# The second convolution's first gathers issued before the last two node tiles' rows are stored, with the head, the seam and the selection rounds reordered

## The chip, the cores and the metric

The kernel runs on one core of a Trainium2 chip. The metric is the device time of one execution in microseconds. The kernel before took 2100.82 us (median of 3 runs, 2099.37 to 2104.38).

## What is computed

A graph network and a feed-forward layer over 6250 nodes of width 256, with 100,000 weighted edges whose destinations are sorted, all in float32. Cut to what matters:

```python
def gcn(x, W, b): return segment_sum(w[:, None] * (x @ W)[src], dst) + b
f1 = layernorm(x)
h  = gcn(f1, W1, b1)                                  # first convolution
z  = leaky(concat([h, f1[root]]))
z  = leaky(gcn(z, W2, b2))                            # second convolution
x  = x + leaky(concat([z, h[root]]) @ Wl + bl)
y  = layernorm(x)
weights = y @ wr + br
sel = top_k(weights, 3125)[:3124]                     # routed nodes
out = x + y; out[sel] += weights[sel] * (gelu(y[sel] @ w1 + b1) @ w2 + b2)
```

## The kernel before

**Tiles and windows.** The nodes lie in 49 windows of 128 (`NW`), the edges in 784 tiles of 128 (`NT`, the last two unused). Four tiles are a group (`TG`), four groups an iteration of 16 tiles (`RING`), and there are 49 iterations (`NIT`) in each of the two convolutions. Both run from the last edges to the first, so from the highest nodes down. For each tile GpSimd gathers the source rows (128 rows of 1 KB) with one indirect DMA (L360) into `ring`, which holds 8 groups. VectorE builds a selection matrix `S` (L1012: destination in the window equals column, times edge weight). TensorE multiplies `S` by the gathered rows and sums a group's four tiles in PSUM (`sums`, L613, `edge_group`), and VectorE adds the sum to the window's slot in `acc` (`add_last`, L1020). Where a group's edges reach into a lower window, an extra sum with `S_more` follows. A float32 product shows as two MATMUL records in the trace.

**Order within a convolution.** POOL may write group g of the ring when `group_used` has reached g - 6 (L355). VectorE raises it once in each group, behind the add of the sum before. `edge_round` is VectorE's part of one iteration, with the selects made two groups ahead; `rounds` on each engine is the loop. The first `first` iterations (here one) are edges alone, then each iteration carries the steps of one finished window, one between each two groups. In the first convolution these are: stage the sums (L433), turn them (L679), multiply by W1 (L703, `ps_h`), bias (L459), leaky (`z_step0`), multiply by W2 (L694, `ps_o`), copy to `rows` (L449) and store to `conv_rows` in HBM (L452), which the second convolution gathers from. In the second they are the same turn, Wl, the residual and layernorm (`x1_step`, `norm_rows`), the router's weight and the FFN's up (L737) and down (L726) products.

**Head.** GpSimd gathers the first 8 groups from the raw `x`; their row statistics are taken (`row_stats`, L952) and the rows scaled in the ring: the first batch (14 tiles) by POOL (L349), the second (16 tiles) by ACT (L414). Meanwhile x is loaded in six chunks (`XCH`), normalised by ACT (L403) and POOL (L345), and stored as `normed_rows` (L286), from which all later gathers of the first convolution read. SyncE then reads the root's row (L293), loads x again (L296, L298) and the late weights Wl, fw1 and fw2 (L304). `fw1s` and `fw2s` (`staged_a`, `staged_b`) are scratch for edges and statistics before. `first_root_row` computes the root's share of the second convolution, between the first iteration and the others.

**Seam.** After the first convolution's last iteration (window 1's and window 0's steps are left, `rounds(..., NW)` and `second_layer(NW)` on TensorE) POOL waits until all rows are stored: `t2_stored` counts 16 at the start and 16 for each store, and L335 wants 16 * (NW + 2). TensorE computes the root terms (L602, L718), VectorE `rootrow` (L1156, L1158).

**Tail.** When the last windows are done, the 3124 largest weights are found by a search in 8 rounds (`ROUNDS`): VectorE counts (L1245, L1246), TensorE adds the counts over partitions (L869). Behind each count TensorE runs pieces of the remaining FFN (`last_ffn`, 26 pieces): two before round 0, one behind rounds 0 and 1, two behind each other, the rest at the end. Then VectorE adds the routed FFN result to the output, from the highest windows down (L1280), and SyncE stores it in 9 chunks (L308); the chunk of windows 2 to 4 waits for the last piece.

## Time and profile before

| | |
|---|---|
| median of 3 runs | 2100.82 us (2099.37 to 2104.38) |
| profiled execution | 2107.75 us, span 2106.0 us |
| TensorE matmul / weight load | busy 1686.5 us (80%) / 1351.4 us (64%) |
| VectorE / ACT | busy 1136.2 us (54%) / 373.3 us (18%) |
| GpSimd (POOL) | busy 1514.8 us (72%) |
| bytes moved | 242 MB, mean 115 GB/s |

```profile
## 2 busy tenths in 40 slices
PE   1588876777767776766689999999998989898886
DVE  8666454444434333333266666665665656555556
POOL 7677777777777777777477777777777777777730
PEclk9999898898988888788699999999999999999998
```

Each digit is the busy share of a slice of 52.7 us in tenths. PE is TensorE, DVE VectorE, ACT ScalarE, PEclk the clock that TensorE was granted. POOL shows 7 nearly everywhere, because its issue between two gathers isn't counted as busy. The seam is the 4 in the middle of POOL's line, the tail the 3 and 0 at its end.

### The profile page before, as it was taken

The page shows a single profiled execution, that of the slowest core. Times are in us where ns is not written, and L with a number is a line of the kernel's source. Part 1 is how long each engine was busy: PE and PEld are TensorE (multiplying, and loading weights), DVE is VectorE, ACT ScalarE, POOL GpSimd, SP SyncE. Part 2 cuts the span into 40 slices and gives each one's busy share as a digit, 9 for nine tenths or more (in the row PEclk, how much of TensorE's full clock was granted, in tenths as well). Part 3 has the DMA queues.
Part 4 walks back from the last instruction along what each step waited for, and adds up shares of the span by engine and source line. Part 5 has one row for each costly group of instructions (what it writes and reads, how often), then busy time and mean ns, then how long its engine had stood idle before and what let it go on. Part 6 is the DMA issues. An engine that isn't in the chain of part 4 may idle for free.

```text
span 2106.0 us, 39360 instructions
## 1 busy us (share of the span) xinstructions
PE 1686.5 (80%) x7147; PEld 1351.4 (64%) x7148; DVE 1136.2 (54%) x4017; ACT 373.3 (18%) x921; POOL 1514.8 (72%) x1609
## 2 busy tenths in 40 slices
PE   1588876777767776766689999999998989898886
PEld 0466655655545555554468888877887777677665
DVE  8666454444434333333266666665665656555556
ACT  6211000001000000000012222222222222222221
POOL 7677777777777777777477777777777777777730
PEclk9999898898988888788699999999999999999998
DMA  8933333333333333333233333333333333333313
GB/s 270 316 112 110 112 110 111 110 110 111 109 112 112 110 112 109 112 112 110 78 105 105 103 105 105 104 103 104 103 105 104 104 105 104 104 104 104 104 57 122
DMA packets 113372, 242.23 MB, mean 115 GB/s; under 512 B 29013, under 2 KB 62740, under 8 KB 113338
## 3 DMA queue, kind: packets, MB, share of 16 engines
q0 software_dynamic: 75200, 205.10, 33.9%
q1 hardware_dynamic: 28444, 29.03, 4.3%
q10 hardware_dynamic: 9694, 7.77, 1.2%
q14 instruction: 27, 0.22, 0.0%
q8 instruction: 7, 0.11, 0.0%
HBM read 222.42 MB, written 19.38 MB: 115 GB/s over the span
## 4 chain that ended last, share of the span: by engine, by line
POOL 44%; PE 25%; issue 18%; DVE 7%; DMA 3%; DVEq 2%; ACT 0%; ACTq 0%; POOLq 0%
POOL ring L360 44%; PE ps_agg L613 15%; PE ps_up L737 3%; PE ps_dn L726 3%; DMA ring<-normed_rows,idx 2%; DMA ring<-conv_rows,idx 1%; DVE S L1012 1%; PE ps_o L694 1%; DVE xs L1280 1%; DVE fw2s L934 1%; DVE acc L1020 1%; PE ps_dn L724 1%; PE ps_o L691 1%; PE ps_o L772 1%; DVE fw2s L952 0%
## 5 line engine op out<-in xcount | busy, mean ns | idle before, releaser
L613 PE MATMUL ps_agg<-ring,S 128*128 x3136 | 863.5, 424 | 363.7 <-DVE S L1012 136.0
L613 PEld LDWEIGHTS ps_agg<-ring,S 128*128 128x128 f32 x3136 | 639.3, 210 | 526.7 <-issue 433.7
L360 POOL DMA_INDIRECT ring<-conv_rows,idx x782 | 747.6, 956 | 256.7 <-issue 232.8
L360 POOL DMA_INDIRECT ring<-normed_rows,idx x752 | 718.0, 955 | 239.6 <-issue 221.0
L1020 DVE TENSOR_TENSOR acc<-acc,ps_agg x490 | 206.4, 421 | 621.5 <-PE ps_agg L613 571.5
L1012 DVE TENSOR_SCALAR S<-iota,dstc,wc 128x128 f32<-128x128 int16 x1584 | 448.7, 363 | 157.3 <-issue 125.8
L613 PE MATMUL ps_agg<-ring,S_more 128*128 x768 | 197.6, 403 | 20.1 <-DVE S_more L1012 13.8
L726 PE MATMUL ps_dn<-fw2s,hT 128*128 128x256 f32 x848 | 209.1, 401 | 0.0
L613 PEld LDWEIGHTS ps_agg<-ring,S_more 128*128 128x128 f32 x768 | 153.4, 204 | 58.7 <-issue 35.5
L726 PEld LDWEIGHTS ps_dn<-fw2s,hT 128*128 128x128 f32 x848 | 163.5, 199 | 40.3 <-issue 18.9
L737 PE MATMUL ps_up<-xnT,fw1s 128*128 128x256 f32 x800 | 183.1, 382 | 1.5 <-ACT hT L471 1.5
L737 PEld LDWEIGHTS ps_up<-xnT,fw1s 128*128 128x128 f32 x800 | 148.1, 190 | 19.7 <-ACT hT L471 1.6
L433 ACT ACTIVATE stage<-acc 128x256 f32 x98 | 40.8, 416 | 426.7 <-DVEq L1046 414.8
L1012 DVE TENSOR_SCALAR S_more<-iota,dmore,wc 128x128 f32<-128x128 int16 x384 | 109.7, 363 | 8.6
L471 ACT ACTIVATE hT<-ps_up,fb1c 128x256 f32<-128x256 f32 (+1 forms) x212 | 82.2, 474 | 67.1 <-PE ps_up L737 67.1
L443 ACT ACTIVATE xnT<-ps_t 128x256 f32<-128x256 f32 x49 | 18.8, 384 | 414.1 <-PE ps_t L679 414.1
L1002 DVE SCALAR_TENSOR_TENSOR zT<-yT 128x256 f32<-128x256 f32 x99 | 42.1, 425 | 39.3 <-DVE acc L1020 31.7
L694 PE MATMUL ps_o<-W2s,zT 128*128 128x256 f32 x200 | 61.2, 432 | 0.3 <-DVE zT L1002 0.3
L459 ACT ACTIVATE yT<-ps_h,b1c 128x128 f32<-128x128 f32 x98 | 30.7, 364 | 155.4 <-PE ps_h L703 153.2
L478 ACT ACTIVATE acc<-ps_dn 128x256 f32 (+1 forms) x53 | 20.4, 384 | 200.2 <-PE ps_dn L726 200.2
L703 PEld LDWEIGHTS ps_h<-xnT,W1s 128*128 128x128 f32 x392 | 53.3, 197 | 3.1
L703 PE MATMUL ps_h<-xnT,W1s 128*128 128x128 f32 x392 | 53.0, 279 | 0.0
(211 smaller groups left out, 1028.3 us busy)
## 6 DMA issues: line engine op xcount, KB each, us to landing
ring<-conv_rows,idx POOLq DMA_INDIRECT x782
ring<-normed_rows,idx POOLq DMA_INDIRECT x752
conv_rows<-rows ACTq DMA_DIRECT2D x50, 128.0 KB
xs<-in_x SPq DMA_DIRECT2D x4, 1280.0 KB, 18.2
normed_rows<-xs SPq DMA_DIRECT2D x3, 1280.0 KB, 6.9
xs<-in_x SPq DMA_DIRECT2D x4, 896.0 KB, 15.7
out_rows<-xs SPq DMA_DIRECT2D x3, 1024.0 KB
xs<-in_x SPq DMA_DIRECT2D x2, 1152.0 KB
```

The source lines that it names most:

```text
L360: pool.indirect_dma_start(out=ring[:, slot * TG + t, :], out_offset=None, in_=rows_of, in_offset=bass.IndirectOffsetOnAxis(ap=idx[:, tile: ...
L433: nc.scalar.activation(stage[:, :], flat(acc[:, ds(slot, 1), :]), ACT.Copy).then_inc(staged[l], 1)
L459: last = nc.scalar.activation(yT[:, k, :], ps_h[:, k * P:(k + 1) * P], ACT.Identity, bias=b1c[:, k:k + 1])
L471: last = nc.scalar.activation(hT[:, b * HB + c, 0:tokens], ps_up[:, c, 0:tokens], ACT.Gelu_apprx_tanh, bias=fb1c[:, b * HB + c:b * HB + c ...
L613: last = nc.tensor.matmul(to, select[:, t, :], moving, start=(t == 0), stop=(t == TG - 1))
L694: last = nc.tensor.matmul(ps_o[:, 0:D], zT[:, k, :], W2s[:, k, :], start=False, stop=(k == KC - 1))
L703: last = nc.tensor.matmul(ps_h[:, c * P:(c + 1) * P], W1s[:, k, c * P:(c + 1) * P], aggT[:, k, :], start=(k == 0), stop=(k == KC - 1))
L726: last = nc.tensor.matmul(ps_dn[:, 0:D], hT[:, c, window * P:(window + 1) * P], fw2s[:, c, :], start=False, stop=(c == HC - 1))
L737: last = nc.tensor.matmul(ps_up[:, c, 0:tokens], fw1s[:, k, (b * HB + c) * P:(b * HB + c + 1) * P], of[:, k, :], start=(k == 0), stop=(k = ...
L1002: return V.scalar_tensor_tensor(to, of, SLOPE, of, ALU.mult, ALU.max)
L1012: last = V.tensor_scalar(to[:, t, :], iota[:, 0:P], at, wc[:, ds(column, 1)], ALU.is_equal, ALU.mult)
L1020: V.tensor_tensor(to, to, flat(ps_agg[:, ds((i + 1) & 1, 1), 0:D]), op=ALU.add).then_inc(acc_step[l], 1)
```

## The change

- **Gathers of the second convolution.** Its ring starts in the half that the first convolution's last iteration doesn't use. The first 14 gathers (`FIRST_TILES`) read through `idx_far`, in which each source below 256 (`NEAR`, windows 0 and 1) is replaced by a zero row, and wait only for the stores down to window 2. Rows of windows 0 and 1 in `conv_rows` are zeroed at the start by three stores from ACT. From group 4 on POOL waits for all stores.
- **Adding the missing rows.** The sources of these edges are loaded to all partitions (`near_src`, 868 KB, on SyncE in the place of the late weights). VectorE makes two one-hot masks of 128 x 1792 in `first_root_row`, one for window 0 and one for window 1. In the seam TensorE multiplies them by the rows of the two windows (28 products), and VectorE adds the results to the 14 ring tiles (`patched`). The first group of the second convolution waits for that. `fw1s` and `fw2s` hold the masks, so they load after the last patch, and TensorE waits for them after the first iteration (`late_weights_in`); Wl loads early.
- **Seam order.** The loops of the first convolution end one window sooner; window 1's product with W2 comes before window 0's turn, and window 0's product goes to `ps_dn` and from there to `row_of_0`. The selects for the second convolution's first two groups come before the patch adds.
- **Head order.** x is loaded and stored in nine chunks instead of six. VectorE makes the first selects before the second batch's row statistics; half of these come before the first iteration, half after it with their factors. The first batch's scaling is shared by POOL (parts 0 and 2) and ACT (parts 1 and 3), with a semaphore for each.
- **Selection.** One FFN piece behind every count instead of one or two.

The diff, cut to its core:

```diff
+        near_src = hT[:, :, :].rearrange("p c n -> p (c n)")[:, 0:FIRST_SPAN]
+        row_of_0 = hT[:, HC - 1, :]
+        near_hot = [staged_a[:, 0:FIRST_SPAN], staged_b[:, 0:FIRST_SPAN]]
...
-        XCH = [(39, NW), (29, 39), (19, 29), (14, 19), (7, 14), (0, 7)]
+        XCH = [(39, NW), (29, 39), (24, 29), (19, 24), (14, 19), (10, 14), (7, 10), (3, 7), (0, 3)]
-        BY_POOL = range(4, len(XCH))
-        STORES = [0, 1, 4, 2, 3, 5]
+        BY_POOL = range(5, len(XCH))
+        STORES = [0, 1, 2, 5, 3, 6, 4, 7, 8]
...
# SyncE
-            for to, of in big_loads[2:]:
+            sp.wait_ge(spread_done, 1)
+            sp.dma_start(near_src[:, 0:E - FIRST_EDGE].bitcast(i32), src[FIRST_EDGE:E].rearrange("(o n) -> o n", o=1).to_broadcast([P, E - FIRST_EDGE])).then_inc(near_loaded, 16)
+            sp.dma_start(*big_loads[2]).then_inc(last_layer_loaded, 16)
+            for done in patched:
+                sp.wait_ge(done, 1)
+            for to, of in big_loads[3:]:
                 sp.dma_start(to, of).then_inc(late_weights, 16)
...
# GpSimd
                 if l == 1:
-                    pool.wait_ge(t2_stored, 16 * (NW + 2))
+                    pool.wait_ge(far_ready, 1)
+                    pool.wait_ge(zero_stored, 16 * 3)
+                    pool.wait_ge(t2_stored, 16 * NW)
...
-                    slot = g % SLOTS
+                    slot = (g + l * QG) % SLOTS
+                    early = l == 1 and it == 0
+                    if early:
+                        pool.wait_ge(group_used[0], NG - SLOTS + q + 2)
+                    if l == 1 and g == QG:
+                        pool.wait_ge(t2_stored, 16 * (NW + 2))
...
# ACT
+            rounds((stage_step0, turned_step0, rows_step0, y_step0), NW - 1)
+            rows_step0(NW - 1)
+            stage_step0(NW - 1)
+            turned_step0(NW - 1)
+            y_step0(NW - 1)
+            act.wait_ge(o_done[0], NW + 2)
+            act.wait_ge(near_ready, 1)
+            nc.scalar.activation(row_of_0, ps_dn[:, 0:D], ACT.Copy).then_inc(o_kept[0], 1)
+            act.wait_ge(o_kept[0], NW + 2)
+            act.dma_start(t2_dram[0:P, :], row_of_0).then_inc(t2_stored, 16)
...
# TensorE
+            pe.wait_ge(near_ready, 1)
+            for q in range(QG):
+                if q >= 2:
+                    pe.wait_ge(patched[q - 2], 1)
+                for t in range(q * TG, min(q * TG + TG, FIRST_TILES)):
+                    bank, half = patch_banks[q & 1][t % TG // 2], t % 2
+                    edges = slice(t * P, (t + 1) * P)
+                    nc.tensor.matmul(bank[:, half * D:(half + 1) * D], near_hot[1][:, edges], rows[:, :], start=True, stop=False)
+                    last = nc.tensor.matmul(bank[:, half * D:(half + 1) * D], near_hot[0][:, edges], row_of_0, start=False, stop=True)
+                    if half:
+                        last.then_inc(patch_done, 1)
...
-                for _ in range(1 if r < 2 else 2):
-                    next(pieces, None)
+                next(pieces)
...
# VectorE
+                if l == 0:
+                    first_selects(0)
+                    for q in range(2):
+                        row_sums(1, q)
                 dve.sem_inc(acc_step[l], 1)
...
+                if l == 0:
+                    with dve.Fori(0, 1) as it:
+                        edge_round(l, it, None)
+                    row_factors(1, [row_sums(1, q) for q in range(2, QG)][-1])
+                    with dve.If(1 < d):
+                        with dve.Fori(1, d) as it:
+                            edge_round(l, it, None)
...
# in first_root_row
+                dve.wait_ge(near_loaded, 16)
...
+                dve.wait_ge(raw_second, 2)
+                for hot, of in zip(near_hot, (lane_at, lane_next)):
+                    last = V.tensor_scalar(hot, near_src.bitcast(i32), zeros[:, 0:1], of, ALU.max, ALU.is_equal)
+                last.then_inc(near_ready, 1)
...
+            first_selects(1)
+            for q in range(QG):
+                tiles = range(q * TG, min(q * TG + TG, FIRST_TILES))
+                dve.wait_ge(landed[1][q], 16 + NIT // 2 * LAND + 16 * len(tiles))
+                for b in range(len(tiles) // 2):
+                    dve.wait_ge(patch_done, 2 * q + b + 1)
+                    held = flat(ring[:, RING + tiles[2 * b]:RING + tiles[2 * b] + 2, :])
+                    last = V.tensor_tensor(held, held, patch_banks[q & 1][b], op=ALU.add)
+                last.then_inc(patched[q], 1)
```

## Rows read from the trace of the kernel before

**Rows 1.** The page: busy time, the chain that ended last, the costliest groups.

```profile
PE 1686.5 (80%) x7147; PEld 1351.4 (64%) x7148; DVE 1136.2 (54%) x4017; ACT 373.3 (18%) x921; POOL 1514.8 (72%) x1609
...
POOL 44%; PE 25%; issue 18%; DVE 7%; DMA 3%; DVEq 2%; ACT 0%; ACTq 0%; POOLq 0%
...
L360 POOL DMA_INDIRECT ring<-conv_rows,idx x782 | 747.6, 956 | 256.7 <-issue 232.8
```

**Rows 2.** Timeline of the head: start us, us, engine, line, operation, operands, count, [idle before].

```profile
57.88 5.32 DVE L952 BATCH_NORM_STATS2 fw2s<-ring 128x6 f32<-128x256 f32 x16
...
67.91 7.97 ACT L414 ACTIVATE ring<-ring,fw2s 128x256 f32<-128x256 f32 x16 [14.35 <-DVEq L958]
69.51 3.17 DVE L1012 TENSOR_SCALAR S<-iota,dstc,wc 128x128 f32<-128x128 int16 x12 [1.69 <-issue]
71.23 6.76 PE L613 MATMUL ps_agg<-ring,S 128*128 x16 [54.05 <-DVE S L1012]
...
75.36 0.42 DVE L1020 TENSOR_TENSOR acc<-acc,ps_agg  x1 [0.92 <-PE ps_agg L613]
...
76.20 0.99 POOL L360 DMA_INDIRECT ring<-normed_rows,idx  x1 [10.73 <-DVEq L1042]
...
78.24 3.09 SPq L298 DMA_DIRECT2D xs<-in_x  x2
...
82.96 0.42 DVE L1020 TENSOR_TENSOR acc<-acc,ps_agg  x1 [0.27 <-issue]
...
85.34 0.41 DVE L1123 COPY rootrow<-ps_dn 1x256 f32<-1x256 f32 x1 [1.21 <-PE ps_dn L602]
...
87.17 0.42 DVE L1020 TENSOR_TENSOR acc<-acc,ps_agg  x1 [0.39 <-issue]
...
91.41 0.95 POOL L360 DMA_INDIRECT ring<-normed_rows,idx  x1 [0.30 <-issue]
```

**Rows 3.** Two source lines: duration ns min/median/max, first and last start us, shapes.

```profile
L916 DVE TENSOR_SCALAR fw1s<-fw1s x1: 693/693/693, 6.0 to 6.0; 98x1024 f32<-98x1024 int32 x1
...
L972 DVE TENSOR_SCALAR hT<-ident,gcol x4: 254/310/477, 14.6 to 15.2; 98x98 f32<-98x98 f32 x4
```

**Rows 4.** Stretches of the head: us, busy by engine, granted clock, DMA share, GB/s.

```profile
96.00:99.00 3.00, 3.00 (x15) 2.26 (x14) 1.83 (x6) 0.77 (x2) 2.09 (x4) 1.00 1.08 356
99.00:102.00 3.00, 3.00 (x19) 2.77 (x18) 1.71 (x6) 0.63 (x2) 2.39 (x3) 1.00 0.62 190
```

**Rows 5.** Timeline of the seam, columns as in rows 2.

```profile
1039.78 0.36 ACTq L452 DMA_DIRECT2D conv_rows<-rows  x1
...
1041.78 0.94 POOL L360 DMA_INDIRECT ring<-conv_rows,idx  x1 [18.69 <-DMA conv_rows<-rows]
...
1049.10 3.78 PE L613 MATMUL ps_agg<-ring,S 128*128 x8 [6.26 <-DMA ring<-conv_rows,idx]
...
1057.39 1.89 PE L613 MATMUL ps_agg<-ring,S_more 128*128 x8
```

**Rows 6.** Stretches of seam and second convolution: PE, PEld, DVE, ACT, POOL, clock, DMA.

```profile
1027.00:1030.00 3.00, 1.70 (x4) 0.79 (x3) 0.42 (x1) 0.23 (x1) 0.00 (x0) 0.50 0.00 0
...
1057.00:1060.00 3.00, 2.28 (x11) 1.67 (x9) 1.74 (x6) 0.00 (x0) 2.39 (x3) 0.99 0.37 98
...
1100.00:1200.00 100.00, 97.36 (x459) 82.63 (x459) 67.53 (x249) 24.92 (x63) 75.92 (x80) 1.00 0.36 104
```

**Rows 7.** Timeline: the add that frees group 24's ring slot, and group 24's gather.

```profile
1138.49 0.42 DVE L1020 TENSOR_TENSOR acc<-acc,ps_agg  x1 [0.28 <-issue]
...
1159.99 0.95 POOL L360 DMA_INDIRECT ring<-conv_rows,idx  x1 [0.30 <-issue]
```

**Rows 8.** Timeline of the tail: a count of round 1, second up, last down.

```profile
2053.79 0.61 PE L869 MATMUL ps_o<-ring,ones 105*128 105x15 f32 x2 [0.44 <-DVE ring L1246]
...
2070.43 3.72 PE L737 MATMUL ps_up<-xnT,fw1s 128*128 128x256 f32 x16 [1.53 <-ACT hT L471]
...
2081.73 19.48 DVE L1280 SCALAR_TENSOR_TENSOR xs<-acc,ring,xs 128x256 f32<-128x256 f32 x49
```

More of the change, by code:

```diff
@@ L347, in _ @@
                         pool.wait_ge(raw_stats, 1)
-                        for t in RAW_TILES[0]:
-                            last = nc.gpsimd.tensor_scalar(ring[:, t, :], ring[:, t, :], raw_rstd[:, t:t + 1], raw_nmr[:, t:t + 1], ALU.mult, ALU.add)
-                            if t % TG == TG - 1 or t == RAW_TILES[0][-1]:
-                                last.then_inc(raw_first, 1)
+                        for part in range(0, QG, 2):
+                            for t in RAW_TILES[0][part * TG:(part + 1) * TG]:
+                                last = nc.gpsimd.tensor_scalar(ring[:, t, :], ring[:, t, :], raw_rstd[:, t:t + 1], raw_nmr[:, t:t + 1], ALU.mult, ALU.add)
+                            last.then_inc(raw_first[part], 1)
                         for stored in f_stored:
@@ L411, in _, with scale_rows @@
             normalise_rows(1)
+            def scale_rows(tiles):
+                for t in tiles:
+                    last = nc.scalar.activation(ring[:, t, :], ring[:, t, :], ACT.Identity, scale=raw_rstd[:, t:t + 1], bias=raw_nmr[:, t:t + 1])
+                return last
+            act.wait_ge(raw_stats, 1)
+            for part in range(1, QG, 2):
+                scale_rows(RAW_TILES[0][part * TG:(part + 1) * TG]).then_inc(raw_first[part], 1)
             act.wait_ge(raw_stats, 2)
-            for t in RAW_TILES[1]:
-                last = nc.scalar.activation(ring[:, t, :], ring[:, t, :], ACT.Identity, scale=raw_rstd[:, t:t + 1], bias=raw_nmr[:, t:t + 1])
+            last = scale_rows(RAW_TILES[1])
             last.then_inc(raw_second, 1)
@@ L708, in _ @@
                 pe.sem_inc(s, 1)
-            rounds(0, (no_step, turn_step0, h_step0, no_step), NW, first_root_term)
-            second_layer(NW)
-            pe.wait_ge(late_weights, 16 * (N_WEIGHTS - 2))
+            rounds(0, (no_step, turn_step0, h_step0, no_step), NW - 1, first_root_term)
+            second_layer(NW - 1)
+            turn_sums(0, NW - 1)
+            h_step0(NW - 1)
+            nc.tensor.matmul(ps_dn[:, 0:D], ones[0:1, :], rootrow[0:1, :], start=True, stop=False)
+            pe.wait_ge(z_ready[0], NW + 1)
+            for k in range(KC):
+                last = nc.tensor.matmul(ps_dn[:, 0:D], zT[:, k, :], W2s[:, k, :], start=False, stop=(k == KC - 1))
+            last.then_inc(o_done[0], 1)
+            pe.wait_ge(o_kept[0], NW + 2)
+            pe.wait_ge(near_ready, 1)
[9 more added lines that the diff above has]
+                        last.then_inc(patch_done, 1)
+            pe.wait_ge(last_layer_loaded, 16)
             pe.wait_ge(root_taken, 2)
@@ L997, in _ @@
             node_stats(1)
-            row_stats(0)
-            row_stats(1)
+            row_factors(0, [row_sums(0, q) for q in range(QG)][-1])
             def leaky(to, of):
@@ L1116, in _ @@
             dve.wait_ge(edges_kept, 3)
+            lane_at, group_at, lane_in, lane_next = (lane[:, i:i + 1] for i in range(4))
             def first_root_row():
```

98 lines of the change are left out of this document (64 added, 34 removed).

## Prediction

> **What bounds the kernel now.** I read the page first. GpSimd (POOL) is 72% busy, nearly all of it in L360: 1564 indirect gathers, one for each tile of 128 edges in each convolution. One is busy for 0.956 us, the next starts 1.26 us after it. TensorE has more busy time, but in the chain of work that ended last POOL holds 44% and TensorE 25% [rows 1]. The timeline of POOL then shows two long gaps: 10.73 us in the head, for a used ring group, and 18.69 us in the seam between the convolutions, for the store of the last conv2 row [rows 2, 5]. Between them it never stops. So the time is: head until the first gather from the normed rows (76.20), 752 gathers, seam, 782 gathers, and a tail of some 79 us. An edit is worth what it moves of POOL's next gather, or takes from head, seam or tail. One thing has to be watched: in 1100 to 1200 TensorE is busy for 97.4 of 100 us [rows 6], so work pushed onto it in the seam can come back as a full ring.
>
> **Part 1, the head.** Removed: the first sums' wait for the statistics of the second raw batch. Added: these statistics and factors between first and second iteration, ACT's scaling behind them, and the mask work in first_root_row. I follow VectorE, which all wait for. The first batch's factors end at 57.9. Before, the selects (69.51) came 1.6 to 1.7 after the second factors (67.9, when ACT starts), so they start at 59.6 now. Eight at 3.17/12 take 2.1 (61.7), eight row statistics at 5.32/16 take 2.7 (64.4), and only then acc_step lets TensorE start. Before, its first group started at 71.23 and the add that waited for it at 75.36, 4.1 later; now that add is at 68.5 and done at 68.9 (before 75.8). POOL follows 0.4 behind: 69.3 instead of 76.20, 6.9 us earlier [rows 2]. The rows are stored by then: SyncE reads one of them at 65.2, and the finer chunks start storing sooner. POOL's six fewer scalings save nothing more, its wait is for the used group.
> That lead doesn't last. Groups 8 to 10 need used-counts of the first iteration, but group 11 needs VectorE's first add of the second. POOL reaches group 11 at 69.3 + 12 x 1.26 = 84.4. VectorE ends the first iteration at 68.9 + (83.4 - 75.8) = 76.5. Then come some 0.6 of loop end, 8 statistics (2.7) and the factors (4.7, from 63.2 to 67.9): 84.5. ACT scales 16 tiles in 7.97 [rows 2]: 92.5. first_root_row now waits for that, because its second mask overwrites the scratch of these factors. Queued behind the wait are, on VectorE, the masks and all selects and adds of the second iteration, and behind these TensorE and group 11. The small operations for indices and lanes fit before 92.5.
> The two masks are tensor_scalars of 128 x 1792 with per-partition scalars. The nearest rows: 1024 columns of int32 with constants took 0.693, 98 float columns with such a scalar 0.254 at best [rows 3]; the selects, 128 columns from int16, follow at 0.264 each [rows 2]. The first two fit about two columns a cycle of 0.96 GHz behind a fixed part, the select fits one. Bounds are 1.0 and 2.0 us for a mask; I take 1.05, since the masks read int32 and write float as L916 does. VectorE goes on at 94.6. From the end of first_root_row (85.75) to the end of the next add (87.59) it was 1.84: 96.4, POOL at 96.8. Group 11 started at 91.41 before [rows 2]. **The head costs 5.4 us**: 12.4 of new waiting against 6.9 gained. Range +4.5 to +11.
> On the masks the Trainium skill, "VectorE: DVE Perf Modes" (section on the perf-mode tier table), says that a float32 tensor_scalar with source and result in SBUF runs at twice the base rate. L972 and L916 agree with it, the int16 selects don't get it. By the selects' rate the sum would be 1.9 us longer.
> The masks also wait for a broadcast load of 868 KB, queued on SyncE behind the second load of x (6.4 MB, issued by 81.3 [rows 2]). Before, three weight loads (2.6 MB) stood there, and they were in at about 99, when the traffic fell from 356 to 190 GB/s [rows 4]. At some 250 GB/s beside the gathers they need 10 us of that, so x is in at some 88 and the broadcast at 91. It hides behind ACT's scaling with 1.5 us of cover; beyond that it costs one for one.
>
> **Part 2, the seam.** The first 14 gathers of conv 2 no longer wait for the last two windows, only for 48 stores, the last issued at 1021.6. A store took 2.0 us from issue (1039.78) to POOL's restart (1041.78) [rows 5]: they start at 1023.6 and end at 1023.6 + 14 x 1.26 = 1041.2. Rows of the last two windows read a zero row instead, at the same cost per gather. From group 4 on POOL waits for all stores. That end is reordered: the product of window 1 (some 3.3 with its ones row, at the low clock) now stands before the turn of window 0, and ACT copies and stores it before it stages window 0. Staging moves 3 us, but window 0's h waited behind that product before, so h moves only 0.8: row 0 is stored at 1040.6 and seen by POOL at 1042.6. The fifteenth gather was at 1041.78 + 17.6 = 1059.4: lead 16.8.
> TensorE has 28 one-hot products to add, from 1040.6. A product is two MATMULs of 256 columns. Eight took 3.78 at 1049 and 1.89 at 1057 [rows 5], so 0.95 or 0.5 a product. The granted clock was 0.50 from 1027 and had risen in 1057 to 1060 [rows 6]. I take 5 us at the lower level (5.3 products) and 22.7 x 0.5 = 11.4: end at 1057.0. Bounds: 14 us (all fast) and 26.6 us (all slow). VectorE's seven adds of 512 columns (0.42 for 256, so some 0.7) run beside it, the last ends 0.8 behind. The Trainium skill, "TensorE: Matmul & The Clock Gate" (Part 1), calls the throttled clock the default, which activity releases; the rows of 1049 and 1057 agree. Without that release the sum is 10 us longer.
> Then the root terms, 3.0 us (before 3.9 at half clock): 1060.0. Four selects and the empty add 1.5, four selects and the next add 1.8: 1063.3. POOL's group 8, which by itself would come at 1042.6 + 20.2 = 1062.8, starts at 1063.7; before, at 1041.78 + 30 x 1.26 = 1079.6. **The seam gives 16.0 us.**
> What is late next? fw1s and fw2s now load after the last patch (1057.8), 2.1 MB beside the gathers: at 356 - 110 = 246 GB/s [rows 4] 8.6 us and 2 of latency, 1068.4; at most 16 us (81.5 to 99 before, with 2.6 MB and a backlog), 1074. TensorE needs them after its first iteration, 5 groups from 1060.3 in some 11.5 us: 1071.8. Hidden by 3.4 us. Then the ring: least slack was at group 24, which started at 1159.99 while the add that frees it ended at 1138.91: 21.1 us [rows 7]. POOL's lead uses 16.0, TensorE's later second iteration up to 4: 20.0. It holds, by one microsecond.
>
> **Part 3, the tail.** One piece of the last FFN behind every count instead of two in rounds 2 to 7. A round with one piece takes 2.94, so the rounds, which ended at 2077.0, end some 3 us sooner; but the pieces of up (L737: 3.72 for two at full clock [rows 8]) now stand in rounds 6 and 7 and hold back the next count by some 1.4. The final adds start near 2080 instead of 2081.73. Sixteen pieces are left instead of ten: from the second up to the end it was 22.8 us (2070.43 to 2093.26), less 1.3 for counts between: 2078.6 to 2100.1. The last 5 windows' adds wait for that and end at 2102.5 instead of 2101.2, but their store is short, while before the span ended 4.8 us behind the last add, for the queue of stores. **I cost the tail at 0**, from -2.6 (clock up throughout) to +2.5 (down through the rounds).
>
> **The sum.** +5.4 - 16.0 + 0 = -10.6. The profiled execution took 2107.75 (span 2106.0 and 1.75 around it), 6.9 more than the median of the runs, 2100.82. So the span should be 2095, the profiled execution 2097, and the median 2100.8 - 10.6 = 2090.2, which I round to 2091.
>
> **The rivals.** First, **the broadcast load is late** and not ACT: it stands behind 6.4 MB, and the gathers start 6.9 us earlier beside it; against it, 1.5 us of cover. It can reach 99: 2090.5 + 6.5 = 2097.
> Second, **slower: the products don't pass**. If TensorE stays at the lower clock and the hand-over of PSUM banks with VectorE makes a product 1.2 us instead of 0.95, 28 take 33.6, end at 1074, and group 8 comes at 1080.5, later than before; the ring's 21.1 us are then used up by TensorE's delay. That is 2100.8 + 5.4 + 0.9 + 1 = 2108. The seam's gain is zero from products that end at 1073. For it: the clock was low for 30 us before 1057 though TensorE worked; against it: it rose once the work closed up.
> Third, **the head is free**: if VectorE's block ended before 84.4, POOL would keep its 6.9: 2100.8 - 6.9 - 16.0 = 2078. That needs 12 us of error in one chain.
> Fourth, **it doesn't do what it says**: POOL isn't released before the last stores. Then only the head's cost is left, 2106. Little in its waits speaks for it.
> Fifth, **the tail's upper end**, 2093.5.
>
> **Chances.** Forecast 0.52 (own range 2085 to 2096), late load 0.14, products 0.12, free head 0.07, no release 0.07, tail 0.08. A measurement here tells about 0.3% (6.3 us) from no change, so faster is under 2094.5, slower over 2107.1. Faster: 0.47 + 0.02 + 0.07 + 0.06 = 0.62. Slower: 0.09 and 0.04 for two of the losses together, 0.13. Same: the rest, 0.25. The range from 2083 to 2106 leaves out the free head and the products.
>
> **What would show it.** Head: first gather from normed rows near 69, then one POOL wait of about 12 us ending near 97, with ACT's 16 scalings just before the two masks; if the masks follow a DMA, the first rival holds, and without a second wait the third. Seam: 14 gathers from 1029, a gap of under 2 us before the fifteenth and of about 1 us before group 8, and 56 MATMULs into ps_up, ps_h and ps_o in 16 to 17 us; if POOL waits for used groups again within 200 us, the 1 us of slack was gone. Tail: counts 2.9 us apart, the last adds waiting for ps_dn. The whole is wrong if gathers start more than 1.26 us apart.

## The result and the profile after

The changed kernel takes **2096.39 us** (median of 10 runs, 2092.58 to 2102.34); the kernel before, beside it, 2100.48 (10 runs, 2098.72 to 2104.38). The ratio is 0.9981, with a 95% interval of 0.9973 to 0.9989: 4.1 us faster, where I had forecast 9.8. The time lies in the range, the sign is right, the size is not: less than half of it came.

The profiled execution took 2095.7 us (span 2094.0). Its page, against [rows 1]:

```profile
PE 1689.6 (81%) x7203; PEld 1359.1 (65%) x7204; DVE 1141.9 (55%) x4030; ACT 375.5 (18%) x927; POOL 1509.1 (72%) x1603
...
POOL 42%; PE 29%; issue 18%; DVE 4%; DMA 4%; DVEq 2%; SPq 1%; ACT 0%; ACTq 0%; POOLq 0%
...
L385 POOL DMA_INDIRECT ring<-conv_rows,idx x768 | 734.6, 957 | 241.7 <-issue 225.4
```

A gather costs what it did, and POOL still leads the chain. TensorE's share of it rose from 25 to 29%, the first sign that POOL waits for it somewhere. The head, against [rows 2] (columns as there):

```profile
68.26 0.98 POOL L385 DMA_INDIRECT ring<-normed_rows,idx  x1 [6.82 <-DVEq L1119]
...
80.63 0.36 SPq L316 DMA_DIRECT2D hT<-in_src  x1
...
83.59 7.96 ACT L444 ACTIVATE ring<-ring,fw2s 128x256 f32<-128x256 f32 x16 [23.47 <-DVEq L1031]
...
90.19 0.15 DVE L1219 CAST lane<-search 128x1 f32<-128x1 int32 x1 [2.85 <-issue]
...
92.30 1.21 DVE L1227 TENSOR_SCALAR fw1s<-hT,vrow,lane 128x1792 f32<-128x1792 int32 x1 [1.77 <-DMA hT<-in_src]
93.43 1.21 DVE L1227 TENSOR_SCALAR fw2s<-hT,vrow,lane 128x1792 f32<-128x1792 int32 x1
94.55 1.11 DVE L1084 TENSOR_SCALAR S<-iota,dstc,wc 128x128 f32<-128x128 int16 x4
95.58 0.41 DVE L1092 TENSOR_TENSOR acc<-acc,ps_agg  x1
...
94.52 0.94 POOL L385 DMA_INDIRECT ring<-normed_rows,idx  x1 [10.62 <-DVEq L1119]
```

The first gather from the normed rows comes 7.9 us earlier, and the eleventh group 3.1 later (94.52 against 91.41). The masks wait for the broadcast load, not for ACT, which is done at 91.55. And POOL starts before the add at 95.58: its release (DVEq) comes from VectorE's queue, ahead of the engine. The seam, against [rows 5]:

```profile
1023.77 0.94 POOL L385 DMA_INDIRECT ring<-conv_rows,idx_far  x1 [0.30 <-issue]
...
1051.56 0.59 PE L777 MATMUL ps_h<-hT,fw1s 128*128 128x256 f32 x2
...
1053.68 0.69 PE L785 MATMUL ps_dn<-rootrow,ones 1*128 1x256 f32 x2 [0.57 <-DVE rootrow L1272]
1057.86 5.79 PE L658 MATMUL ps_agg<-ring,S 128*128 x16 [3.48 <-DVE acc L1092]
...
1062.30 0.95 POOL L385 DMA_INDIRECT ring<-conv_rows,idx  x1 [1.27 <-DVEq L1119]
```

The gap of 18.69 us is gone, and group 8 comes at 1062.30 instead of 1079.70. Then, against [rows 7], where no wait stood:

```profile
1080.26 3.78 PE L658 MATMUL ps_agg<-ring,S_more 128*128 x8 [3.75 <-DVE S_more L1084]
...
1085.75 5.51 PE L793 MATMUL ps_dn<-fw2s,hT 128*128 128x256 f32 x16
...
1094.02 0.94 POOL L385 DMA_INDIRECT ring<-conv_rows,idx  x1 [1.80 <-DVEq L1119]
1111.48 0.94 POOL L385 DMA_INDIRECT ring<-conv_rows,idx  x1 [1.63 <-DVEq L1119]
1132.51 0.94 POOL L385 DMA_INDIRECT ring<-conv_rows,idx  x1 [1.18 <-DVEq L1119]
1149.54 0.42 DVE L1092 TENSOR_TENSOR acc<-acc,ps_agg  x1 [0.28 <-issue]
1149.85 0.95 POOL L385 DMA_INDIRECT ring<-conv_rows,idx  x1 [2.57 <-DVEq L1119]
```

POOL waits for used groups: 7.0 us in five waits between 1090 and 1150, of which four stand here (each number in brackets holds the usual 0.30 of issue). The DVE line is the add that frees group 24's slot, and the gather below it is group 24's. In the tail the counts are 2.94 us apart, and the span ends 77.6 us behind the last gather instead of 79.5.

### The profile page after: what moved, and what is told of

It reads as the page before. It is cut to its first block, busy times and chain, and to the rows that moved or that the text cites. A ratio compares the mean times of both kernels' runs of the same rounds, so it can differ in the third digit from the quotient of the medians.

```text
span 2094.0 us, 39574 instructions
## 1 busy us (share of the span) xinstructions
PE 1689.6 (81%) x7203; PEld 1359.1 (65%) x7204; DVE 1141.9 (55%) x4030; ACT 375.5 (18%) x927; POOL 1509.1 (72%) x1603
## 4 chain that ended last, share of the span: by engine, by line
POOL 42%; PE 29%; issue 18%; DVE 4%; DMA 4%; DVEq 2%; SPq 1%; ACT 0%; ACTq 0%; POOLq 0%
POOL ring L385 41%; PE ps_agg L658 16%; PE ps_dn L793 4%; PE ps_up L804 4%; DMA ring<-normed_rows,idx 2%; DVE S L1084 1%; DMA ring<-conv_rows,idx 1%; PE ps_o L743 1%; PE ps_dn L791 1%; SPq L312 1%; PE ps_o L839 1%; DVE acc L1092 1%; DMA hT<-in_src 1%; PE ps_o L740 1%; DVEq L1092 0%
## 5 line engine op out<-in xcount | busy, mean ns | idle before, releaser
L658 PE MATMUL ps_agg<-ring,S 128*128 x3136 | 852.7, 421 | 333.9 <-DVE S L1084 87.7
L385 POOL DMA_INDIRECT ring<-conv_rows,idx x768 | 734.6, 957 | 241.7 <-issue 225.4
L470 ACT ACTIVATE stage<-acc 128x256 f32 (+1 forms) x98 | 40.8, 416 | 410.1 <-DVEq L1123 403.6
L1074 DVE SCALAR_TENSOR_TENSOR zT<-yT 128x256 f32<-128x256 f32 x99 | 42.1, 425 | 40.5 <-DVE acc L1092 31.0
L743 PE MATMUL ps_o<-W2s,zT 128*128 128x256 f32 x196 | 57.3, 416 | 0.0
## 6 DMA issues: line engine op xcount, KB each, us to landing
xs<-in_x SPq DMA_DIRECT2D x6, 640.0 KB, 15.6
```

The source lines that it names most:

```text
L385: pool.indirect_dma_start(out=ring[:, slot * TG + t, :], out_offset=None, in_=rows_of, in_offset=bass.IndirectOffsetOnAxis(ap=at, axis=0)) ...
L470: nc.scalar.activation(stage[:, :], flat(acc[:, ds(slot, 1), :]), ACT.Copy).then_inc(staged[l], 1)
L658: last = nc.tensor.matmul(to, select[:, t, :], moving, start=(t == 0), stop=(t == TG - 1))
L743: last = nc.tensor.matmul(ps_o[:, 0:D], zT[:, k, :], W2s[:, k, :], start=False, stop=(k == KC - 1))
L1074: return V.scalar_tensor_tensor(to, of, SLOPE, of, ALU.mult, ALU.max)
```

## The experiments

For the study I cut every profiled execution at POOL's gathers: head up to group 11; the 740 gathers from there to the last of the first convolution; seam from that gather to group 8 of the second; from there to the last gather; tail. The waits are those for used groups between group 8 and 1160 us. (after_again, masks_at_seam and half_products have one more, of 1.3 us, between 1232 and 1239.) All in us, from starts in POOL's timeline:

| kernel | group 11 | 740 gathers | seam | to last gather | waits | tail | span |
|---|---|---|---|---|---|---|---|
| before | 91.4 | 930.7 | 57.6 | 946.8 | 0 | 79.5 | 2106.0 |
| after | 94.5 | 928.0 | 39.8 | 954.0 | 7.0 | 77.6 | 2094.0 |
| before_again | 90.9 | 929.6 | 57.3 | 945.8 | 0 | 82.7 | 2106.4 |
| after_again | 95.9 | 929.0 | 40.6 | 956.5 | 8.8 | 77.4 | 2099.5 |
| before_light | 90.9 | 929.6 | 54.6 | 945.8 | 0 | 79.5 | 2100.5 |
| before_light_2 | 90.9 | 929.3 | 54.8 | 945.2 | 0 | 78.9 | 2099.1 |
| after_light | 94.9 | 929.6 | 39.7 | 953.9 | 7.0 | 77.6 | 2095.6 |
| half_products | 97.3 | 930.8 | 41.7 | 949.3 | 0 | 78.4 | 2097.4 |
| seam_alone | 96.0 | 930.7 | 40.7 | 947.9 | 0 | 77.4 | 2092.8 |
| root_early | 95.5 | 929.4 | 40.6 | 948.8 | 2.1 | 77.6 | 2091.9 |
| filler | 95.0 | 929.9 | 41.5 | 949.0 | 2.8 | 78.5 | 2094.1 |
| root_filler | 95.7 | 930.6 | 41.5 | 947.7 | 1.1 | 77.4 | 2092.9 |
| masks_root | 94.5 | 930.1 | 41.9 | 948.4 | 2.9 | 78.7 | 2093.6 |
| masks_at_seam | 95.8 | 930.4 | 42.1 | 957.5 | 8.0 | 82.8 | 2108.5 |
| tail_alone | 90.9 | 930.5 | 54.8 | 946.0 | 0 | 80.8 | 2103.0 |
| old_head | 91.1 | 932.5 | 41.0 | 950.8 | 2.3 | 80.2 | 2095.5 |
| old_head_best | 91.2 | 933.1 | 42.1 | 949.7 | 0 | 78.4 | 2094.6 |
| one_loop | 88.2 | 930.5 | 41.9 | 947.9 | 0.7 | 77.0 | 2085.4 |

A row shows one execution, and some stand off their kernel's median: masks_at_seam's is 7.4 us over it, old_head's 4.2, old_head_best's 7.9, and seam_alone's 5.2 under. The study's runs were taken in four sessions on three chips, each time beside the kernel before (medians 2100.62 to 2101.38); every ratio is to the kernel before of the same session, and across sessions the ratios compare better than the medians.

**Controls.** The first kernels that I made assert the bounds of the table values that TensorE and VectorE load. before_again and after_again show what that alone costs:

```diff
-v = within(pe.value_load(wtab[...]), (NW + 1) << CBITS)
+v = pe.value_load(wtab[...], min_val=0, max_val=(NW + 1) << CBITS)
```

> The kernel before, with the bounds of the table values that TensorE and VectorE load asserted (two short register instructions beside each of the 392 loads), as in all kernels of this study. Neither engine sets POOL's pace in the middle, so it should stand within 3 us of the kernel before, 2098 to 2104 us. The question is the profiled execution: the one of before took 2107.75 us against a median of 2100.8. If that was one slow execution, this profile is near 2100 us and its gathers of the first convolution run at 1.255 us from start to start instead of 1.259; if profiling itself costs 7 us, it is near 2107 again, and the 12 us between the two profiled executions are what the change brings.

> The changed kernel with the same assertions. If the change is worth the 4 us of the medians, it stands 3 to 5 us under before_again, ratio 0.998, with POOL's waits for used groups between 1090 and 1150 us again at 7 us in sum. If it is worth the 12 us that the profiled executions show, the ratio is 0.994.

before_again took 2104.4 us, ratio to before 1.0011 (1.0002 to 1.0020); after_again 2103.73, 1.0006 (0.9995 to 1.0018). By the medians the assertions cost the changed kernel 7 us and before 3 to 4; by the ratios 5 and 2. With them the change is worth 0.7 us, where 3 to 5 was expected. Of the 5.5 us between the spans of after_again and after, 1.4 stand in the head and 2.5 behind group 8. So I went on with a lighter guard, in all kernels below but half_products and masks_at_seam:

```diff
+v = within(pe.snap(pe.value_load(wtab[...]) & 0xFFFF), (NW + 1) << CBITS)
```

> The changed kernel with a lighter form of the same guard: the loaded table value is masked to 16 bits, one register instruction instead of two beside each load. The assertions of after_again cost 7 us against the changed kernel itself (2103.7 against 2096.4); the gap of VectorE ahead of its root step in the head grew from 0.7 to 6.6 us, and the waits for used groups in the second convolution from 7 to 10 us. With half the added instructions I expect half of that, 2099 to 2101 us. If it is the length of the code near the head's branches that matters and not the number of register instructions, it can come anywhere between 2096 and 2104.

> The kernel before with the light guard (one masking instruction beside each load of a table value), the partner of after_light. I expect it within 1.5 us of the kernel before itself, 2099.5 to 2102.5. Second question: both profiled executions of the kernel before so far took 7 and 4 us more than its median. If that is chance (the gathers' pace between 1.2558 and 1.2595 us, the tail between 77.4 and 82.8), this one may land anywhere in 2098 to 2106; if the profile always catches it slow, it is again 4 to 7 us over its median.

> The kernel before_light once more, for its profile. Its seam came in two lengths: 18.4 us of gap in before and before_again, with TensorE's clock at 0.50 from 1026 to 1045, and 15.3 and 15.6 in before_light and tail_alone, with the clock at 0.75 to 1.00 there. If it is chance, either may come; if the guard's form sets it, the gap is 15.3 again. The median should be 2101 to 2103.

before_light: 2102.14 us, 1.0001 (0.9991 to 1.0010), and again 2101.93, 1.0009; after_light: 2097.72, 0.9986 (0.9977 to 0.9995), less than the 2099 to 2101 expected. The pair stands 4.4 us apart by the medians and 3.2 by the ratios, against 4.1 for before and after, and is the fair one to cut up. It also shows that the seam of the kernel before has two lengths. POOL's restart in before_light, and two stretches 1025 to 1040 (us, busy by engine, granted clock, DMA), of before_light and then of before:

```profile
1037.07 0.94 POOL L360 DMA_INDIRECT ring<-conv_rows,idx  x1 [15.60 <-DMA conv_rows<-rows]
```

```profile
1025.00:1040.00 15.00, 9.13 (x34) 5.64 (x32) 5.09 (x18) 2.22 (x7) 2.32 (x3) 0.86 0.08 26
```

```profile
1025.00:1040.00 15.00, 12.54 (x32) 7.79 (x33) 1.64 (x5) 2.19 (x6) 0.00 (x0) 0.54 0.03 9
```

With TensorE's clock at 0.86 on the mean the gap is 15.6 us, at 0.54 it is 18.7. before and before_again had the long seam (18.7 both), before_light twice and tail_alone the short one (15.6, 15.8 and 15.9, clock 0.86, 0.84 and 0.77). The execution on which I based the forecast was one of the long ones.

**What fills the ring.** In half_products the 14 tiles get one product each, in root_early the root step moves ahead, in filler TensorE is kept busy:

```diff
-matmul(bank[...], near_hot[1][:, edges], rows[:, :], start=True, stop=False)
-last = matmul(bank[...], near_hot[0][:, edges], row_of_0, start=False, stop=True)
+last = matmul(bank[...], near_hot[0][:, edges], row_of_0, start=True, stop=True)
```

> The changed kernel with one product for each of the 14 first tiles instead of two: the rows of window 1 are left out of them, so the result lacks their part; the gathers, the waits and all the rest stay. Theory: the 7 us that POOL waits for used groups in the second convolution come from VectorE's first adds there, 8.8 us later than before (1062.4 against 1053.6), because they stand behind the products. Fourteen products less are 6 to 7 us of TensorE (28 took 14 us), so the adds come 6 us sooner, POOL's waits shrink from 7 to 1 or 2 us, and the whole is 5 to 6 us shorter than after_again. Rival: the later rounds of the second convolution, each with a piece of the last layers, are what uses up the ring, whenever they start; then the waits stay at 5 to 7 us and the time within 2 us of after_again.

half_products took 2098.20 us, 0.9980 (0.9971 to 0.9990): 5.5 under after_again, and the waits of 8.8 us before 1160 are gone. TensorE's work ahead of the first adds fills the ring, but this run doesn't show how much of it. Counted from POOL's group 8, VectorE's ninth add (the empty one counted) ends after 18.2 us instead of 23.2, which is the products. The tenth ends 6.0 us behind the ninth instead of 9.1, and there the clock differed too: 0.83 in 1080 to 1090, in after_again 0.73, and 0.76 in the ten us after.

```diff
 pe.wait_ge(o_kept[0], NW + 2)
+pe.wait_ge(root_taken, 2); root_term(Wls)
 ...  # products of group 0
+pe.wait_ge(rootrow_ready, 2)
+matmul(ps_dn[:, 0:D], ones[0:1, :], rootrow[0:1, :]).then_inc(root_done, 1)
 ...  # products of groups 1 to 3
```

> As after_light, but the root terms of the second convolution stand ahead of the products on TensorE, and the two copies of their row on VectorE ahead of the first two groups of patch adds, instead of behind them all. In the changed kernel 6.1 us lie between the last product (1051.8) and the first matmul of the second convolution (1057.9). Theory: half_products took the products' 7 us off and POOL's waits for used groups fell from about 10 to 2.6 us, so what counts is when VectorE's first adds come; the root step's chain of five handovers is 3 to 4 us of that, and taken out it gives 3 to 4 us of the waits back: ratio to before 0.0015 to 0.002 lower than after_light's. Rival: TensorE only gets idle later, in the second iteration, or the patch adds of group 0 wait for the root row and hold back the banks; then under 1 us.

root_early took 2094.76 us, 0.9974 (0.9963 to 0.9985), 3.0 under after_light and 0.0012 in the ratio, where 0.0015 to 0.002 was expected. Its last product, its first sums, and the one long wait that POOL has left:

```profile
1055.56 0.59 PE L780 MATMUL ps_h<-hT,fw1s 128*128 128x256 f32 x2
1056.91 1.99 PE L658 MATMUL ps_agg<-ring,S 128*128 x8 [0.76 <-DVEq L1154]
```

```profile
1148.34 0.94 POOL L385 DMA_INDIRECT ring<-conv_rows,idx  x1 [2.36 <-DVEq L1120]
```

The chain of 6 us between products and sums is down to 1. Here too the clock takes a part: counted from group 8 the ninth add ends after 20.7 us instead of 23.1 in after_light, and the tenth 5.9 us behind it instead of 8.6, with the clock at 0.83 in 1080 to 1090 instead of 0.55.

```diff
+def keep_clock():
+    with pe.If(s < 1):
+        for _ in range(7):
+            nc.tensor.matmul(ps_o[:, 0:D], ident[:, :], zeros[:, :], start=True, stop=True)
```

> after_light with seven dummy products of 256 columns (3.0 us at the full clock, into a bank that nobody reads then) on TensorE, once, in the second group of the first round with a last-layer step, where TensorE idled for 3.75 to 3.96 us from 1076.5 on and the granted clock then stood at 0.50 to 0.55 for some 10 us. Theory: that fall of the clock is 4 to 5 us of VectorE's delay (eighth to tenth add 9.2 us apart in the changed kernel, 4.1 in seam_alone, whose clock stayed at 1.00 and whose POOL never waited). With TensorE kept busy the clock stays up, POOL's waits for used groups between 1080 and 1160 fall from 7.0 to 3 us or less, and the whole is 3 to 4 us shorter than after_light. Rival: the clock falls for another reason, or the dummy products push back the group behind them by as much; then the waits stay at 6 to 8 us.

filler took 2095.11 us, 0.9967 (0.9955 to 0.9979), 2.6 under after_light. The dummy products and the step behind them, then the stretch 1080 to 1090 of filler and of the changed kernel:

```profile
1080.82 3.19 PE L692 MATMUL ps_o<-vrow,ident 128*128 128x256 f32 x14
...
1087.85 3.72 PE L800 MATMUL ps_dn<-fw2s,hT 128*128 128x256 f32 x16
```

```profile
1080.00:1090.00 10.00, 9.04 (x43) 7.45 (x42) 7.33 (x31) 1.09 (x3) 7.56 (x9) 1.00 0.36 102
```

```profile
1080.00:1090.00 10.00, 9.74 (x25) 7.60 (x26) 5.30 (x23) 1.09 (x2) 7.59 (x8) 0.53 0.37 107
```

At a clock of 1.00 the 16 matmuls take 3.72 us instead of 5.51. The ninth add comes as late as in after_light (23.0 and 23.1 us behind group 8), the tenth 4.6 us behind it instead of 8.6, and the waits fall from 7.0 to 2.8: the clock's fall behind the idle stretch had cost 4.0 us. The median fell by 2.6 where 3 to 4 was expected. seam_alone, below, shows such an execution without dummy products.

> root_early and filler together. root_early left 2.1 us of POOL's waits for used groups, with its clock at 0.83 in 1080 to 1090. If the waits have the two causes named, root step and clock, they are gone here altogether, and the time is 1 to 2 us under root_early's and 6 to 8 under before: ratio 0.9965 to 0.997. If it isn't under root_early, something else than TensorE's lateness holds POOL.

root_filler took 2093.67 us, 0.9961 (0.9947 to 0.9974), 1.1 us of waits left. Both causes together are nearly all of them. Against filler, with the clock at 1.00 in 1080 to 1090 in both, the ninth add comes 1.7 us sooner behind group 8 (21.3 against 23.0) and the waits are 1.7 us less: so much the root step brings, with the clock of its own idle stretch in it (0.83 in 1055 to 1075 in filler, 0.91 in root_filler). Without the two causes the kernel stands 8 us under before, near the 9.8 forecast.

**The head.** seam_alone puts back the old order of chunks, statistics and scaling:

> The changed kernel with the order of the head undone: six chunks of x as before, both batches of statistics and factors ahead of the first selects, POOL scaling all of the first batch. The masks stay in the head, and the seam and the selection are those of the change. Theory: the first normed gather goes back from 68 to 76 us, but the lead was lost again by the eleventh group anyway (94.5 against 91.4), which now waits for the broadcast load and the masks alone: group 11 between 93 and 95, and the whole within 2 us of after_light. Rival: the load isn't late without the early gathers beside it, group 11 comes at 91.5 to 92.5, and the whole is 2 to 4 us shorter than after_light, so that the reordered head is what takes a part of the gain.

Its first mask, its group 11 and its stretch from 1080 to 1090 (timelines and windows, columns as above):

```profile
93.83 1.21 DVE L1215 TENSOR_SCALAR fw1s<-hT,vrow,lane 128x1792 f32<-128x1792 int32 x1 [7.60 <-DMA hT<-in_src]
```

```profile
96.05 0.94 POOL L385 DMA_INDIRECT ring<-normed_rows,idx  x1 [5.47 <-DVEq L1117]
```

```profile
1080.00:1090.00 10.00, 6.83 (x32) 5.86 (x33) 7.56 (x32) 1.19 (x3) 7.65 (x8) 1.00 0.39 107
```

It took 2099.73 us, 0.9995 (0.9985 to 1.0004), 2.0 over after_light, at the edge of what was expected; the two intervals overlap. So with the masks in the head, the new order of the head gains 2 us at most. The load was later than expected (93.8), VectorE stood 7.6 us at it, and group 11 came at 96.0 instead of 93 to 95. By chance its profile shows TensorE's clock up in 1080 to 1090 and no waits for used groups; it was the fastest of its 11 runs, the median is 5 us above.

masks_at_seam moves the masks with their waits to the end of the first convolution:

```diff
 rounds(0, (z_step0, no_step, zero_step0, no_step), NW - 1, ..., first_root_row)
+dve.wait_ge(near_loaded, 16)
+...
+for hot, of in zip(near_hot, (lane_at, lane_next)):
+    last = V.tensor_scalar(hot, near_src.bitcast(i32), zeros[:, 0:1], of, ALU.max, ALU.is_equal)
```

> The changed kernel with the two masks, and the waits for the broadcast load and for the scaled raw rows, taken out of the head and put on VectorE ahead of the last turn of the first convolution, where it has idle time. Theory: POOL's second wait in the head (10.6 us, until 94.5) hangs on ACT's scaling, the masks and the selects behind them in one chain. Without the masks (2.4 us, with their gap 3) and with the first iteration's end no longer behind the load (0.7 us), group 11 starts 3 to 4 us sooner, near 91, and the whole is 3 to 4 us shorter than after_again, since the ring's stalls in the second convolution start from the seam and move along. Rival: the scaling by ACT alone sets it, since TensorE waits for it anyway; then group 11 moves by the masks' 2.4 us at most, and if the masks at the seam delay the last store, half of that is lost again.

A miss: 2102.88 us, 1.0006 (0.9995 to 1.0017), 0.9 under after_again. Group 11 in masks_at_seam, then in after_again:

```profile
95.76 0.95 POOL L385 DMA_INDIRECT ring<-normed_rows,idx  x1 [12.28 <-DVEq L1119]
```

```profile
95.95 0.95 POOL L385 DMA_INDIRECT ring<-normed_rows,idx  x1 [12.59 <-DVEq L1119]
```

Two masks less, 2.4 us of VectorE, moved POOL by 0.2. In both kernels the small operations ahead were done at 93.1 to 93.2; from there VectorE's queue took 2.6 to 2.8 us to reach the report of the used group, with masks or without. What counted was when the small operations came, and those stood behind a gap: 6.6 us of VectorE ahead of the root step. (In the changed kernel itself that gap is 0.7, another of 2.85 stands behind the root step, and the load came last, at 92.3.)

> root_early with the masks at the end of the first convolution, as in masks_at_seam. There group 11 of the head came at 95.8 against 95.9 with the masks in the head: the 2.4 us of masks cost 0.2, because VectorE's queue, which reports the used groups, needs 2.5 us for the instructions behind them in any case. In this lighter form VectorE may reach the masks earlier than the broadcast load, as in the changed kernel (waits 1.8 us for it, until 92.3): then the head gains 1 to 2 us over root_early. Rival: the gap of VectorE without a cause in the profile (2.9 and 6.6 us so far) takes it, and nothing is gained.

masks_root took 2096.48 us, 0.9979 (0.9969 to 0.9989), no better than root_early, the gap still there:

```profile
88.90 0.16 DVE L1075 SCALAR_TENSOR_TENSOR root_in<-rootcol 128x2 f32<-128x2 f32 x1 [6.50 <-issue]
```

one_loop is masks_root with filler and without code that these edges never run:

```diff
 row_factors(1, [row_sums(1, q) for q in range(2, QG)][-1])
-with dve.If(1 < d):
-    with dve.Fori(1, d) as it:
-        edge_round(l, it, None)
```

> masks_root with filler, and without the second copy of VectorE's loop over the rounds without steps (its range is empty for these edges, so nothing that runs is left out, only the code that is jumped over). In after_light, root_early, masks_root and root_filler VectorE stands still for 6.5 us between the factors' last step (82.4 to 83.2) and the root step (89 to 89.7), and the profile names no cause. Theory: that is the fetch of its instructions behind the jump, while 6.4 MB of x are loading; without the copy the gap is under 1.5 us, the root step comes at 83 to 84, and group 11 of the head at 88 to 90. TensorE's second iteration still waits for ACT's scaling (91.4), so group 12 is what counts: 95 to 96 instead of 100, and the whole 3 to 5 us under masks_root. Rival: VectorE waits for something else there (the root column's load); then the gap stays at 6 us and nothing is gained.

Its root step, and POOL's waits in the head:

```profile
82.60 0.16 DVE L1082 SCALAR_TENSOR_TENSOR root_in<-rootcol 128x2 f32<-128x2 f32 x1 [0.15 <-DVE fw2s L1003]
```

```profile
88.20 0.94 POOL L385 DMA_INDIRECT ring<-normed_rows,idx  x1 [4.84 <-DVEq L1127]
95.36 0.94 POOL L385 DMA_INDIRECT ring<-normed_rows,idx  x1 [2.35 <-DVEq L1127]
100.76 0.94 POOL L385 DMA_INDIRECT ring<-normed_rows,idx  x1 [0.67 <-DVEq L1127]
```

2089.00 us, 0.9945 (0.9931 to 0.9959): 7.5 under masks_root, of which filler is a part, and 4.7 under root_filler. The gap fell from 6.5 to 0.15, group 11 comes at 88.2, and the next groups lose 2.4 us again (2.05 and 0.37 over the usual 0.30), behind sums that TensorE starts at 91.2, when ACT's scaling has ended at 90.5. What is shown is that the stall goes with the second copy; seam_alone, old_head and old_head_best, which have no second copy either, stand for 0.65 us there. But the jump alone doesn't make it: the changed kernel has the copy and stood for 0.7. That VectorE fetches its instructions there is my reading, and the transfers speak for it. This line of masks_root, 86 to 88 us, is missing in one_loop's same stretch (columns: packets, MB, share):

```profile
q14 instruction: 1, 0.01, 1.4%
```

It doesn't name the engine. The changed kernel has such a packet in its gap of 2.85 us, from 88 to 89.5.

> seam_alone (the head's order undone) with the masks and their wait for the broadcast load at the end of the first convolution. In seam_alone VectorE stood at that wait from 86.2 to 93.8 and group 11 came at 96.0. Theory: the load and the masks are the whole loss of the head there, so group 11 comes at 90.9 as in before_light, 5 us sooner, and the whole is 3 to 4 us shorter than seam_alone, since the masks at the seam delay its fifteenth gather by 1 us (masks_root against root_early: 41.9 against 40.6 us from the last gather of the first convolution to group 8). Rival: the ring of the second convolution takes it: POOL waits for used groups again, as it did in the changed kernel and didn't in seam_alone's profile, and the time stays within 1.5 us of seam_alone's.

> old_head with root_early and filler. If the terms add: head 4 us better than root_filler's (95.7 to 91.0, less 1 at the seam), the ring's waits at 1 to 2 us: 2089 to 2091 us, ratio to before 0.9945, against 0.9961 for root_filler. If the reordered head with its early first gathers is worth something that group 11 doesn't show, it is no better than root_filler.

old_head took 2093.08 us, 0.9964 (0.9952 to 0.9976), 6.7 under seam_alone where 3 to 4 was expected, with group 11 at 91.1 instead of 96.0; where the rest comes from was not found. old_head_best took **2088.45 us** (5 runs, 2086.99 to 2096.35), 0.9941 (0.9927 to 0.9954), half a us less than expected: the fastest here, 12 us under before and 8 under the changed kernel. Its profiled execution is the slowest of the five: the 740 gathers took 933.1 us there, at 1.254 us from start to start in the median, where all others but old_head have 1.251 or 1.252. It equals one_loop within its interval, and unlike that one it serves any edges.

**The tail.**

```diff
-for _ in range(1 if r < 2 else 2):
-    next(pieces, None)
+next(pieces)
```

> The kernel before with nothing of the change but one piece of the last layer behind every count. My forecast put the tail at 0 (from -2.6 to +2.5 us). The profiled changed kernel had 77.65 us behind its last gather, before 79.51. Theory: 1.5 to 2.5 us gained, ratio to before 0.999 with before_light at 1.000. Rival: the tail varies by 5 us by itself (82.75 and 82.78 in before_again and masks_at_seam), so nothing is gained in the mean, ratio as before_light's within 0.0005.

2101.72 us, 0.9997 (0.9988 to 1.0006), tail 80.8 against 79.5 and 78.9 in before_light: alone the edit brings nothing that can be told, as its rival had it. The changed kernel's 77.6 is 1.3 to 1.9 shorter than those; where that comes from was not found.

## Why the prediction was right in sign and wrong in size

**The sum, term by term**, from before_light to after_light: head +4.0, the 740 gathers 0, seam -14.9, from group 8 to the last gather +8.1, tail -1.9; together -4.7, for 4.9 in the spans and 4.4 in the medians. The forecast had +5.4, 0, -16.0, 0, 0. The stretch from group 8 to the last gather misses by more than the 5.9 between the two sums.

**The ring: the step that failed.** "It holds, by one microsecond" had 21.1 us of slack and 20.0 used, 16.0 by POOL's lead and "up to 4" by TensorE's later second iteration. Measured: POOL's lead at group 8 was 17.4 (1079.7 to 1062.3), and the add that frees group 24 ended at 1150.0 instead of 1138.9, 11.1 later. 28.5 less 21.1 is 7.4, and POOL waited 7.0. The pair before_light and after_light gives the same: a lead of 11.1, the add 14.6 later (1151.8 against 1137.2), a slack of 18.5, so 7.2 too little, and 7.0 of waits. The return of these waits was one of the signs that the prediction named. The 11.1 us of the add have two parts. 6.7 were there by the ninth add (1084.9 against 1078.2): products, root step and first sums. I had VectorE's first such add at 1063.3 (it ended at 1062.4), but put no row of before beside it, where it ended at 1053.6. The ring step then used 4 for what the step above it had made nearly 10. root_filler against filler shows the root step's share of this part, 1.7 us; half_products and root_early show the part too, mixed with the clock. The other 4.4 came between the ninth and the tenth add: TensorE idled for 3.75 us at 1076.5, and its clock stood at 0.53 in the 1080s. I had looked for the clock at the products only, not behind them. filler shows this part.

**The seam.** The products ran from 1038.1 to 1052.1, where I had 1040.6 to 1057.0: row 0 was there earlier, and the clock was up from 1041.6 on. Products in the wrong state, my rival for a loss, didn't occur. VectorE's first adds came where forecast all the same, since the root step and the start of the sums took 6 us where I had 3, and the first sums began at a clock of 0.50 (1055.3 to 1062.1), where I had the full one. The seam itself gave 17.8 against the profiled execution, but 14.9 against the usual one, because the gap of 18.69 [rows 5] is the long of two lengths. The terms were made against an execution 7 us over the median, and I shifted the sum by these 7 without asking in which stage they lay: 3.0 of the 5.5 us between the spans of before and before_light are the seam, which the change takes away in either case.

**The head.** The mechanism was right, first gather at 68.3 (forecast 69.3), then one wait until 94.5 (forecast 96.8), and two of its terms were off. First, the load and not ACT ended last, by 0.75 us (92.30 against 91.55): the first rival, by a small margin. Second, I let POOL follow the add behind the masks, 2.2 us after VectorE goes on; the release comes from its queue, 0.1 before the second mask ends. Masks of 1.13 us from start to start agree with the 1.05 taken. The Trainium skill, "VectorE: DVE Perf Modes" (the perf-mode tier table), gives a float32 tensor_scalar in SBUF twice the base rate. The masks read int32 and write float32, and the trace agrees: 1792 columns in 1.13 us, where one a cycle at the 0.96 GHz that it states would be 1.87.

**The rest.** The late weights were issued at 1053.0 and not waited for. The tail at 0 stands within what can be measured. POOL was released early, so the fourth rival fell, and the third with the wait of 10.62.

## What to carry to other kernels

When an edit pulls an engine ahead, the cover it uses up is its own lead plus the lateness of the one that frees its buffers; put each of the two beside a row of before, and take no margin of 1 us as held. Behind every new idle stretch of TensorE, read the granted clock of the 10 us after it. Before a term is taken from a profile, see whether the execution is at the median, and if not, in which stage it differs.

## What the runs showed of the hardware

VectorE's queue runs ahead of its engine: a count it reports reached POOL 1.1 us before the add ahead of it began (94.52 and 95.58), and taking 2.4 us of masks out ahead of it moved POOL by 0.2. In masks_root a loop's second copy, which is jumped over, came with a stall of VectorE of 6.5 us while x was loading, and one_loop without it stood for 0.15. TensorE idle for 3.75 and 3.96 us (after, after_light) was followed by a clock of 0.53 and 0.55 in 1080 to 1090, idle for 3.75 and 3.84 us (half_products, root_early) by 0.83, and idle for 3.52 us (seam_alone) by 1.00: the length of the idle stretch alone didn't tell. The fall to 0.55 cost 4 us of lead. A guard of two register instructions at each table load cost the changed kernel 5 to 7 us; one of a single instruction some 1, which the intervals don't tell from nothing.
